# A two-layer decoder on one core: normalisation, transfer and filler steps moved in a hand-written order

## The chip, the cores and the metric

The kernel runs on one core of a Trainium2 chip. The metric is the device time of one execution in microseconds (us), lower is better. The core has five engines with a queue each, which run side by side and wait for each other by semaphores: TensorE (PE; its weight loads are shown as PEld), VectorE (DVE), ScalarE (ACT), GpSimd (POOL), and SyncE (SP), which here only issues transfers.

## The reference

Eight sequences of 112 tokens with 512 features go through two pre-normalised layers, all in float32. In outline:

```
x = x + L0_attn(layernorm(x))        # 32 query heads, 8 key heads, rotary, a sink logit per head
x = x + L0_xattn(layernorm(x), mask, ctx)   # own attention with a mask, and 375 context rows, gated
x = x + L0_ffn(layernorm(x))         # router: 8 experts, the best 2 for each token, weighted
x = x + L1_attn(layernorm(x))        # 16 query heads, 4 key heads, low-rank keys and values, anchors
x = x + L1_xattn(layernorm(x), ctx)  # softmax over the context, readout
x = x + L1_ffn(layernorm(x))         # sigmoid/tanh/sine features, two rounds of products and norms
```

In layer 1 the values are `h @ Wv_down.T @ Wv_up.T + v_anchor` and the attention output is multiplied by `Wo`. In the router the logits are `rsqrt(mean(x^2)) * x @ router_logits`, and the two largest choose the experts.

## The kernel before, in words

The 896 tokens are held as 7 tiles of 128 tokens (`NT`), and as 4 units of 2 sequences (`NU`). A Python list, `build_order()`, is the order of the whole program. A step is a tuple such as `("kq1", 0, 5)`, and each engine runs its own part of each step in the list's order: TensorE its products, VectorE and ScalarE the reading of PSUM, GpSimd some sums, SyncE the loads. Nothing reorders at run time. An instruction that waits holds up all that is behind it on its engine. `place()` goes through the list and gives each product one of the eight PSUM banks, the longest unused; the product then waits until the last reader of that bank has finished.

Steps that matter here:

- `stats`, `scale`, `turn` are a layer norm: mean and variance on VectorE (lines 1516 to 1520), the power -0.5 on GpSimd (L2251), the scaling on VectorE (L1529), the transposes on TensorE (L1053), their copy on ScalarE (L2041). In layer 0 a `scale` of a later tile also brings a bias sum `bo` on GpSimd (L2256).
- Layer 0 attention, `attend0`: `s0` scores, `m0` maxima, `p0` transposes of the weights (their copies on VectorE are L1589), `v0` values (L1119), `d0` sums. `spread` puts the projections of the next unit, `kq0` and `vp0`, between them.
- Cross attention, `attendx` and `cross`: for each sequence and group of heads `xk` computes shifted context scores (L1209); it needs the query with the maximum added, which is `mt` (a transpose on TensorE, L1199, then a sum on VectorE, L1641). `ce` are the exponentials on ScalarE (L2109), `xcv` the products with the values (L1239), `xu` the copy (L2121), `xd` and `xn` the division on VectorE (L1649 to L1666). `xw` is the output product of a tile (L1247).
- `ent` steps (L1459) are products of two weight matrices that depend on no token. They are laid where TensorE would wait. Those of layer 0 stand at the end of the cross attention, around the router (`route`, `lt`, `rank`) and before the experts.
- Router: `lt` needs a small power on GpSimd (L2331), beside eight memsets (L2330). After `rank` the tokens are scattered by transfer (`put`), and the experts' rows are loaded.
- After the experts, `get` gathers each tile's two expert rows by an indirect transfer (L2347), `mix` adds them to x on VectorE (L1827).
- Layer 1 attention: `kq1` are the eight query projections of a unit (L1381), read by VectorE (L1545) and summed by GpSimd; `ba`, `wp`, `bb` (the list `absorb()`) multiply the value-up matrix and the anchor into the output weights (L1365, L1355). `attend1` holds `s1` (scores, L1394), `c1` (L1842, L1848, exponentials L2161), `p1` (transposes; copies L2169 on ScalarE and L1864 on VectorE), `v1` (values, L1414; copies L2175 and L1870), `w1` (output, L1426). `td`, `vp1`, `ku` (L1330, L1346, L1338) are the low-rank projections.
- Loads of layer 1: `w1q` n is slot n of the query weights (1 MB, for `kq1` 2n and 2n+1), `w1o` n one quarter of the output weights (1 MB). SyncE issues `w1q` 1 when the gathers of tile 1 have landed, waits until those of tile 3 have landed, issues `w1q` 2, and then the four `w1o`.

## Time and profile before

| what | value |
|---|---|
| median of 3 runs | 1756.43 us (1752.63, 1756.43, 1756.64) |
| the profiled execution, its own time | 1756.78 us |
| its span on the core | 1754.5 us, so 2.3 us lie around it |
| TensorE busy | 1700.0 us, 97% |
| VectorE, ScalarE, GpSimd busy | 56%, 31%, 26% |
| granted TensorE clock, mean | 0.996 |
| moved from and to HBM | 155.46 MB read, 16.52 MB written |

TensorE is busy nearly all the time, so the table says little of where time could be won: one has to look for the few stretches in which TensorE waits, and for those in which its clock is granted at half. A row of the timeline has the start, the length, the engine, the line, what is written and read, the number of instructions, and in brackets the idle time before it with what ended it. The trace counts a float32 product as two matmul records: a step of 16 products shows as x32.

### The profile page before, as it was taken

The numbers are of one execution on the slowest core, as the hardware profiler recorded it, in microseconds if no ns is written. First come the engines' busy times: TensorE is split into PE (matmuls) and PEld (weight loads), VectorE is DVE, ScalarE is ACT, GpSimd is POOL, SyncE is SP. The second block draws the span as 40 slices with busy tenths as digits, with TensorE's granted clock in tenths as the row PEclk, the third lists the DMA queues.
The fourth block names the chain that finished last, engine by engine and source line by source line (L and its number), as shares of the span: only waits on it lengthen the run. The fifth ranks groups of instructions, "written<-read, shape, count | busy, mean of one in ns | idle before, by whom it ended". The sixth has DMA issues, their size and how long they took to land.

```text
span 1754.5 us, 32913 instructions
## 1 busy us (share of the span) xinstructions
PE 1700.0 (97%) x13868; PEld 1137.6 (65%) x13868; DVE 986.4 (56%) x1901; ACT 548.0 (31%) x1515; POOL 458.5 (26%) x549
## 2 busy tenths in 40 slices
PE   7999999999999999999999999998999999999998
PEld 6876666657666666666546888877677775444444
DVE  3765556437777777677743111116554555664987
ACT  0343333524444444445410111110422222333411
POOL 2532323512222213222113000005231210002676
PEclk9999999999999999999989999999999999999999
DMA  9100012000000000000147988866000033752101
GB/s 394 49 1 1 1 43 73 1 27 19 13 8 19 4 17 20 8 13 1 67 171 294 347 334 335 335 231 229 2 1 1 1 137 129 241 189 84 29 14 42
DMA packets 31987, 172.26 MB, mean 98 GB/s; under 512 B 4024, under 2 KB 4024, under 8 KB 18176
## 3 DMA queue, kind: packets, MB, share of 16 engines
q1 hardware_dynamic: 29600, 162.82, 24.9%
q0 software_dynamic: 2240, 7.34, 1.2%
q8 instruction: 109, 1.79, 0.4%
q14 instruction: 38, 0.31, 0.1%
HBM read 155.46 MB, written 16.52 MB: 98 GB/s over the span
## 4 chain that ended last, share of the span: by engine, by line
PE 86%; DVE 10%; POOL 1%; issue 1%; ACT 1%; DMA 1%; POOLq 0%; DVEq 0%; ACTq 0%
PE PS L1312 9%; PE PS L1080 7%; PE PS L1131 6%; PE PS L1381 5%; PE PS L1459 5%; PE PS L1169 5%; PE PS L1490 4%; PE PS L1321 4%; PE PS L1426 4%; PE PS L1192 3%; PE PS L1209 3%; PE PS L1477 3%; PE PS L1139 3%; PE PS L1156 2%; PE PS L1161 2%; DVE R L1618 2%
## 5 line engine op out<-in xcount | busy, mean ns | idle before, releaser
L1312 PEld LDWEIGHTS PS<-R,W 128*128 128x128 f32 x1344 | 153.2, 192 | 11.7 <-issue 11.7
L1312 PE MATMUL PS<-R,W 128*128 128x128 f32 x1344 | 153.6, 275 | 2.2 <-DVE R L1811 2.2
L1634 DVE TENSOR_REDUCE nmw<-PS 112x2 f32<-112x750 f32 x128 | 114.1, 934 | 42.5 <-PE PS L1192 42.5
L2251 POOL TENSOR_TENSOR rstd<-veps,mhalf 128x1 f32<-128x1 f32 (+1 forms) x71 | 53.8, 757 | 307.2 <-DVE veps L1520 284.0
L1080 PE MATMUL PS<-xT,W 128*128 128x224 f32 x640 | 127.8, 360 | 1.0 <-ACT xT L2041 0.7
L1080 PEld LDWEIGHTS PS<-xT,W 128*128 128x128 f32 x640 | 122.2, 194 | 9.9 <-issue 7.6
L1818 DVE TENSOR_TENSOR R<-R,PS 128x512 f32<-128x512 f32 x21 | 14.5, 688 | 199.1 <-PE PS L1312 199.1
L1459 PE MATMUL PS<-W 128*128 128x512 f32 x256 | 119.8, 611 | 0.9 <-ACT R L2109 0.9
L2109 ACT ACTIVATE R<-PS 125x672 f32<-125x672 f32 x128 | 86.6, 730 | 85.8 <-PE PS L1209 85.8
L2277 POOL TENSOR_TENSOR R<-R 128x224 f32<-128x224 f32 x80 | 52.8, 661 | 223.4 <-DVE R L1545 116.6
L1381 PE MATMUL PS<-xT,W 128*128 128x224 f32 x512 | 101.9, 359 | 2.5 <-DVE R L1545 2.2
L1490 PE MATMUL PS<-W,xT 128*128 128x512 f32 x224 | 100.7, 593 | 0.9 <-ACT xT L2046 0.9
L1381 PEld LDWEIGHTS PS<-xT,W 128*128 128x128 f32 x512 | 97.2, 193 | 5.1 <-DVE R L1545 2.5
L1131 PE MATMUL PS<-W,R 128*32 128x512 f32 (+1 forms) x512 | 99.1, 594 | 0.0
L2057 ACT ACTIVATE R<-PS,small 112x112 f32<-112x112 f32 x256 | 87.0, 386 | 34.0 <-DVE small L1569 34.0
L1602 DVE TENSOR_TENSOR x<-x,PS 128x512 f32<-128x512 f32 x35 | 24.1, 687 | 120.0 <-PE PS L1131 69.2
L1459 PEld LDWEIGHTS PS<-W 128*128 128x128 f32 x256 | 48.7, 195 | 55.5 <-issue 52.6
L2347 POOL DMA_INDIRECT R<-ys_rows,R x14 | 13.4, 958 | 245.9 <-DMA ys_rows<-R 241.6
L2271 POOL TENSOR_TENSOR R<-R,small 112x448 f32<-112x448 f32 x32 | 42.8, 1336 | 132.0 <-DVE small L1580 132.0
L1426 PE MATMUL PS<-W,R 128*32 128x512 f32 (+1 forms) x384 | 74.8, 594 | 0.7 <-DVE R L1870 0.7
L1321 PE MATMUL PS<-W,R 128*128 128x512 f32 x168 | 75.4, 592 | 0.0
L1131 PEld LDWEIGHTS PS<-W,R 128*32 128x32 f32 (+1 forms) x512 | 35.7, 130 | 60.9 <-issue 60.9
(306 smaller groups left out, 3325.3 us busy)
## 6 DMA issues: line engine op xcount, KB each, us to landing
W<-in_we SPq DMA_DIRECT2D x63, 1024.0 KB, 8.0
R<-in_ctxT SPq DMA_DIRECT2D x12, 750.0 KB, 7.3
W<-in_entwT SPq DMA_DIRECT2D x8, 1024.0 KB, 7.0
W<-in_entpw SPq DMA_DIRECT2D x8, 1024.0 KB, 8.3
R<-in_ctx SPq DMA_DIRECT2D x8, 750.0 KB
xs_rows<-in_x SPq DMA_DIRECT2D x3, 1792.0 KB, 36.1
R<-xs_rows SPq DMA_DIRECT2D x21, 256.0 KB, 8.3
ys_rows<-R SPq DMA_DIRECT2D x21, 256.0 KB, 8.5
```

The costliest lines, as they stand in the source:

```text
L1080: o = e.matmul(PS[:, m, ab * UT:(ab + 1) * UT], lw, xT[:, k, tok], start=k == 0, stop=k == 3)
L1131: o = e.matmul(PS[to, m, :], OT[:, g, c, of], Wo[:, g * 8 + c, :], start=c == 0, stop=c == 7)
L1169: o = e.matmul(PS[0:KC, m, 0:256], CT[b % 2][:, k, t * KC:(t + 1) * KC], Wx[2][:, k, 256 * g:256 * g + 256], start=k == 0, stop=k == 3)
L1312: o = e.matmul(PS[:, m, c * 128:(c + 1) * 128], gate_up(j % 3, k, off + c * 128), BT[:, j % 2, k, :], start=k == 0, stop=k == 3)
L1321: o = e.matmul(PS[:, m, :], GA[:, j % 2, k, :], W[:, GROUPS[j % 3][2], k * D:(k + 1) * D], start=k == 0, stop=k == 3)
L1381: o = e.matmul(PS[:, m, ab * UT:(ab + 1) * UT], Wlq[c // 2][:, c % 2, k, ab * 128:ab * 128 + 128], xT[:, k, tok], start=k == 0, stop=k == 3)
L1426: o = e.matmul(PS[to, m, :], LOT[:, g, c, of], Wlo[2 * g + c // 3][:, c % 3, :], start=c == 0, stop=c == 5)
L1459: o = e.matmul(PS[:, m, :], W[:, wt, kk * D + m * 128:kk * D + (m + 1) * 128], W[:, pw, kk * D:(kk + 1) * D], start=k in starts, stop=k + ...
L1490: o = e.matmul(PS[:, m, :], xT[:, k, tcol(t)], wk[:, k, :], start=k == 0, stop=k == 3)
L1634: e.tensor_reduce(nmw[0:S, par, :].rearrange("p (r f) -> p r f", r=4)[:, r:r + 2, 16 - 16 * par], PS[0:S, r:r + 2, 0:SC], AX.X, ALU.max, n ...
L2057: e.activation(SS[0:S, z, k * S:k * S + S], PS[0:S, r, bcol(j)], ACT.Exp, bias=sm[:, 1, k:k + 1], accum_out=sm[:, 4, k:k + 1])
L2109: e.activation(p_of(b, c, par)[0:KC, r:r + 2, :], PS[0:KC, r:r + 2, 0:3 * S], ACT.Exp).then_inc(*up("cexp", (b, c, par, r)))
```

## The change

Five places of the order move; each instruction that computes something is still there, except that the two-step `xw` has two waits in the place of one.

1. Layer 0 attention: `scale` of tiles 4, 5 and 6 come later, between the projections, and no longer directly behind their `stats`.
2. End of the cross attention: the last `mt` comes ahead of `xd`; only one `ent` step in the place of three stands between the last values and the output product; the output product of tile 6 waits for the last piece only before its fourth product; `scale` of tile 5 comes behind the output product. The `ent` steps that were ahead now stand behind `rank`.
3. Router: GpSimd's power comes ahead of its eight memsets.
4. Start of layer 1: `w1o` 2 and 3 are issued right behind `w1q` 1, ahead of the wait for the gathers; `ba` and the first `wp` come ahead of the transposes of tiles 2 and 3, and the next two `wp` between `kq1` 5 and 6.
5. Layer 1, unit 1: the norm of tile 6 comes behind `c1`, no longer between `s1` and `c1`.

The diff, without its context:

```
-        out += runs[n]
+        final = n == 16 * NBATCH - 1
+        out += runs[n][:-1] + [("mt", *pieces_of(n // 4), 1)] + runs[n][-1:] if final else runs[n]
...
-        if n % 4 == 3:
+        if n % 4 == 3 and not final:
...
-    at_end = {("xk", 7, 3, 1): h[:1], ("xcv", 7, 3, 1): h[1:4], ("xd", 7, 3): [("scale", 2, 5)], ("xw", 6): h[4:5] + [("turn", 2, 5)] + h[5:6] + [("route", 1)]}
+    at_end = {("xk", 7, 3, 1): h[:1], ("xcv", 7, 3, 1): h[1:2], ("xw", 6): [("scale", 2, 5)] + h[2:3] + [("turn", 2, 5)] + h[3:4] + [("route", 1)]}
...
-    ... ("route", 2), ("lt",)] + part([3]) + [("rank",)]
-    out += part(range(4, FRONT)) + ...
+    ... ("route", 2), ("lt",)] + part([2]) + [("rank",)]
+    out += part(range(3, FRONT)) + ...
...
 def pace1(step):
+    if step[0] in ("stats", "scale"):
+        return 0.0
...
-            nxt = norms(0, bs) + nxt[:4] + turns(0, bs) + nxt[4:]
+            nxt = [("stats", 0, b) for b in bs] + nxt[:1] + [("scale", 0, bs[0])] + nxt[1:2] + [("scale", 0, b) for b in bs[1:]] + nxt[2:4] + turns(0, bs) + nxt[4:]
...
-    out += [("load", "w1q", 1), ("mix", 0), ...
-    out += [("load", "w1q", 2)] + [("load", "w1o", n) for n in range(4)] + ...
+    out += [("load", "w1q", 1), ("load", "w1o", 2), ("load", "w1o", 3), ("mix", 0), ...
+    out += [("load", "w1q", 2)] + [("load", "w1o", n) for n in range(2)] + ...
...
-    out += kq[3:4] + [("mix", 5)] + kq[4:5] + turns(3, (2, 3))
-    out += [("mix", 6)] + kq[5:7] + once[:4] + begin[:-1] + kq[7:] + begin[-1:] + [("load", "mu", 0)]
+    out += kq[3:4] + [("mix", 5)] + kq[4:5] + once[:2] + turns(3, (2, 3))
+    out += [("mix", 6)] + kq[5:6] + once[2:4] + kq[6:7] + begin[:-1] + kq[7:] + begin[-1:] + [("load", "mu", 0)]
...
-            nxt = norms(3, bs) * (u > 0) + nxt[:5] + turns(3, bs) + nxt[5:]
+            nxt = nxt[:5] + turns(3, bs) + nxt[5:]
...
+        steps = [s for n in range(2 * (u == 0), 4) for s in attend1(4 * u + n)]
+        if u and u + 2 < NU:
+            k = steps.index(("c1", u, 0, 1)) + 1
+            steps[k:k] = norms(3, bs)
+        out += spread(steps, nxt, pace1)
...
                 w.wait_ge(*at("d_q3", "wx"))
-                for b in (t, t + 1):
-                    w.wait_ge(*at("oxt", (b, 3)))
-                xw_part(t, m, range(4)).then_inc(*up("attended", ("xw", t)))
+                w.wait_ge(*at("oxt", (t, 3)))
+                if t == NT - 1:
+                    w.wait_ge(*at("oxt", (t + 1, 2)))
+                    xw_part(t, m, range(3))
+                w.wait_ge(*at("oxt", (t + 1, 3)))
+                xw_part(t, m, range(3 * (t == NT - 1), 4)).then_inc(*up("attended", ("xw", t)))
...
             def ba():
-                w.wait_ge(*at("d_w1o", 3))
+                w.wait_ge(*at("d_w1o", 1))
...
             def lt():
                 w.wait_ge(*at("var", 0))
+                e.tensor_tensor(rt[:, 8, 8:8 + NT], rt[:, 8, 0:NT], mhalf[:, 0:NT], ALU.pow).then_inc(*up("rms", 0))
                 for n in range(8):
                     e.memset(rsl(rt, 9)[:, :, n:n + 1], 8.0 - n).then_inc(*up("rank", n))
-                e.tensor_tensor(rt[:, 8, 8:8 + NT], rt[:, 8, 0:NT], mhalf[:, 0:NT], ALU.pow).then_inc(*up("rms", 0))
```

The `ba` step waits for all four `w1o` loads before and now, since they count up one semaphore; only the last in order is another. Line numbers of the changed kernel are 7 to 10 higher from the output product on.

TensorE at the start of layer 1. Before, the transposes of tiles 2 and 3 (`xn` into PS, 8 transposes) follow the five projections, and `ba` (`W,col`) and `wp` (`W` alone) come behind two more projections:

```order
L1381 MATMUL PS<-xT,W 128x224 x40
L1053 MATMUL PS<-cst,xn 128x128 x8
L1381 MATMUL PS<-xT,W 128x224 x16
L1365 MATMUL PS<-W,col 32x512 x16
L1355 MATMUL PS<-W 32x512 x12
L1394 MATMUL PS<-R 112x112 x16
```

The same stretch in the changed kernel:

```order
L1391 MATMUL PS<-xT,W 128x224 x40
L1375 MATMUL PS<-W,col 32x512 x16
L1365 MATMUL PS<-W 32x512 x4
L1060 MATMUL PS<-cst,xn 128x128 x8
L1391 MATMUL PS<-xT,W 128x224 x8
L1365 MATMUL PS<-W 32x512 x8
L1391 MATMUL PS<-xT,W 128x224 x8
L1404 MATMUL PS<-R 112x112 x16
```

Twenty products moved ahead of the transposes and eight between the projections; the sum of the stretch is the same.

VectorE at the end of the cross attention, from the division of the last group but one (`xd`) on. Before, the sum with the query (L1641, `R,PS` 128x112) stands behind the four instructions of the division:

```order
L1649 TENSOR_SCALAR R<-R,cst 128x224
L1651 SCALAR_TENSOR_TENSOR R<-R,cst 128x224
L1654 STREAM_SHUFFLE R<-R 128x224
L1656 RECIPROCAL R<-R 128x224
L1641 TENSOR_TENSOR R<-R,PS 128x112
```

In the changed kernel it stands ahead of them:

```order
L1651 TENSOR_TENSOR R<-R,PS 128x112
L1659 TENSOR_SCALAR R<-R,cst 128x224
L1661 SCALAR_TENSOR_TENSOR R<-R,cst 128x224
L1664 STREAM_SHUFFLE R<-R 128x224
L1666 RECIPROCAL R<-R 128x224
```

One instruction changed its place with four.

VectorE at the first scores of unit 1 of layer 1. Before, the norm of tile 6 (its last instruction is the scaling, `xn<-x,mv,rstd`) stands ahead of the reading of the scores (L1842) and of a copy for TensorE (L1864):

```order
L1516 BN_STATS st<-x 128x6
L1518 BN_AGGR mv<-st 128x2
L1520 TENSOR_SCALAR veps<-mv 128x1
L1529 TENSOR_SCALAR xn<-x,mv,rstd 128x512
L1842 TENSOR_TENSOR R<-PS,cst 112x896
L1864 COPY R<-PS 112x448
```

In the changed kernel:

```order
L1852 TENSOR_TENSOR R<-PS,cst 112x896
L1874 COPY R<-PS 112x448
L1858 TENSOR_REDUCE ls<-R 112x8
L1860 TENSOR_SCALAR ls<-ls 112x8
L1526 BN_STATS st<-x 128x6
L1528 BN_AGGR mv<-st 128x2
L1530 TENSOR_SCALAR veps<-mv 128x1
L1539 TENSOR_SCALAR xn<-x,mv,rstd 128x512
```

The four instructions of the norm went behind the four that read the scores and the transposed weights.

## Rows read from the trace of the kernel before

**Rows 1.** Part 1 of the page: busy time, share, instructions of each engine.
```profile
PE 1700.0 (97%) x13868; PEld 1137.6 (65%) x13868; DVE 986.4 (56%) x1901; ACT 548.0 (31%) x1515; POOL 458.5 (26%) x549
```

**Rows 2.** Timeline, layer 0 attention: start, length, engine, instruction [idle before].
```profile
72.09 1.41 DVE L1529 TENSOR_SCALAR xn<-x,mv,rstd 128x512 f32<-128x512 f32 x1 [0.52 <-POOL rstd L2251]
...
74.09 0.97 PE L1119 MATMUL PS<-R 112*64 112x448 f32 x4 [1.30 <-DVE R L1589]
```

**Rows 3.** Timeline, end of the cross attention and the router.
```profile
882.02 0.32 PE L1199 MATMUL PS<-cst,nmw 112*128 112x112 f32 x1
...
884.92 0.21 DVE L1641 TENSOR_TENSOR R<-R,PS 128x112 f32<-128x112 f32 x1
...
885.18 0.92 PE L1209 MATMUL PS<-R 32*125 32x112 f32 x24 [0.82 <-DVE R L1641]
...
886.98 3.78 PE L1459 MATMUL PS<-W 128*128 128x512 f32 x4 [0.88 <-ACT R L2109]
...
892.11 0.54 ACT L2121 ACTIVATE R<-PS 128x448 f32<-128x448 f32 x1 [4.56 <-PE PS L1239]
...
896.24 0.34 DVE L1666 SCALAR_TENSOR_TENSOR R<-R,tg 128x112 f32<-128x112 f32 x1
...
904.96 0.35 POOL L2330 MEMSET R<- 128x7 f32 x8 [1.12 <-DVE R L1686]
```

**Rows 4.** Windows: stretch, length, busy by engine, granted clock, DMA share, GB/s.
```profile
882.20:886.20 4.00, 2.36 (x65) 1.63 (x64) 3.52 (x9) 1.34 (x3) 2.17 (x3) 1.00 0.20 84
886.20:893.10 6.90, 6.12 (x30) 2.74 (x31) 0.38 (x2) 1.89 (x3) 0.00 (x0) 0.51 0.01 4
...
910.10:913.50 3.40, 3.40 (x5) 1.32 (x4) 2.89 (x14) 0.05 (x1) 0.00 (x0) 0.51 1.00 422
...
1220.70:1224.20 3.50, 3.50 (x11) 3.18 (x10) 3.46 (x5) 0.00 (x0) 1.82 (x3) 0.51 0.02 7
```

**Rows 5.** Timeline, start of layer 1.
```profile
1199.81 15.40 PE L1381 MATMUL PS<-xT,W 128*128 128x224 f32 x80
...
1216.70 0.66 PE L1053 MATMUL PS<-cst,xn 128*128 128x128 f32 x4 [1.05 <-DVE R L1545]
...
1218.38 1.14 DVE L1545 TENSOR_TENSOR R<-PS,cst 128x448 f32<-128x448 f32 x2
...
1219.58 8.01 PE L1381 MATMUL PS<-xT,W 128*128 128x224 f32 x32 [2.22 <-DVE R L1545]
...
1227.52 3.64 PE L1365 MATMUL PS<-W,col 128*32 128x512 f32 x32
...
1230.97 2.82 PE L1355 MATMUL PS<-W 128*32 128x512 f32 x24
```

**Rows 6.** SyncE's issues, and DMA from 1188 to 1222: packets, windows, us to landing.
```profile
1188.82 11.61 SPq L2406 DMA_DIRECT2D W<-in_w1q  x2
...
DMA packets 738, 3.39 MB, mean 212 GB/s; under 512 B 126, under 2 KB 126, under 8 KB 522
...
1212.00:1216.00 4.00, 3.65 (x21) 3.36 (x20) 3.34 (x9) 0.32 (x1) 2.68 (x5) 1.00 1.02 424
...
1218.00:1222.00 4.00, 2.42 (x9) 2.28 (x10) 3.96 (x7) 0.00 (x0) 1.76 (x3) 0.84 0.32 78
...
W<-in_w1q SPq DMA_DIRECT2D x1, 1024.0 KB, 8.4
R<-ys_rows,R POOLq DMA_INDIRECT x8, 8.8
```

**Rows 7.** Timeline, layer 1, first scores of unit 1.
```profile
1294.31 4.95 POOL L2261 TENSOR_TENSOR x<-x,R 128x512 f32<-128x512 f32 x4
...
1299.87 0.55 DVE L1529 TENSOR_SCALAR xn<-x,mv,rstd 128x512 f32<-128x512 f32 x1 [5.34 <-POOL rstd L2251]
...
1302.00 0.78 PE L1414 MATMUL PS<-R 112*32 112x112 f32 x24 [1.12 <-DVE R L1864]
...
1306.65 1.02 PE L1346 MATMUL PS<-W,xT 128*112 128x96 f32 x8 [1.25 <-ACT R L2175]
```

More of the change, by code:

```diff
@@ L403, in experts @@
 def experts():
-    out = [("load", "front", 3), ("load", "we", 0), ("load", "w1s", 0), ("scale", 2, 6), ("turn", 2, 6), ("route", 2), ("lt",)] + part([3]) + [("rank",)]
-    out += part(range(4, FRONT)) + [("ea", 0, k) for k in range(FRONT)] + [("put", t) for t in range(NT)]
+    out = [("load", "front", 3), ("load", "we", 0), ("load", "w1s", 0), ("scale", 2, 6), ("turn", 2, 6), ("route", 2), ("lt",)] + part([2]) + [("rank",)]
+    out += part(range(3, FRONT)) + [("ea", 0, k) for k in range(FRONT)] + [("put", t) for t in range(NT)]
     out += [("load", "experts", 0), ("load", "rows", 0), ("load", "we", 1), ("load", "rows", 1), ("load", "rows", 2), ("load", "we", 2)]
@@ L579, in build_order @@
             out += norms(3, (4, 5)) + once[4:10] + second + once[10:]
-        out += spread([s for n in range(2 * (u == 0), 4) for s in attend1(4 * u + n)], nxt, pace1)
+        steps = [s for n in range(2 * (u == 0), 4) for s in attend1(4 * u + n)]
[3 more added lines that the diff above has]
+        out += spread(steps, nxt, pace1)
     out += [("load", "c5", 0), ("load", "c5", 1), ("mu",)]
```

4 lines of the change are left out of this document (2 added, 2 removed).

## The prediction, as put on record before the run

> **What bounds the kernel now.** I read the page's busy shares first. TensorE works 1700.0 us of a 1754.5 us span, 97% [rows 1], so 54.5 us are all that any reordering can win, and some of those lie at the start and the end. Then I went through TensorE's waits in order of time, since in a stream as full as this each wait that goes moves all that is behind it, unless the next wait grows by as much. Third I read the granted clock by windows, as a busy TensorE at half clock is lost time too, which no list of waits shows. The reader is to see two things: the changed places are exactly places where TensorE waits 0.8 to 2.2 us for an engine whose queue holds something less urgent in front [rows 2, 3, 5, 7]; and just behind two of them the clock is granted at 0.51, the lower of its levels (1.2 in the place of 2.4 GHz) [rows 4].
>
> **Layer 0, scaling between the projections.** TensorE's values wait 1.30 us for a VectorE copy. In front of that copy stand two scalings, the second of which starts at 72.09 and takes 1.41 us, up to 73.50, and TensorE goes on at 74.09 [rows 2]. Without them the copy comes more than 1.4 us sooner, so the whole 1.30 goes. The scalings now run between projections. There VectorE follows TensorE and the transposes that need them stand four projections later. With each goes a sum of 128x512 on GpSimd, 1.24 us by the four of that shape in 4.95 us [rows 7]; it may hold up one rotary sum by less than that, hidden by the 3.08 us that a projection takes (five in 15.40 us) [rows 5]. Bounds: a gain of 0 to 1.30; I take 1.30. The move of tile 6 meets no wait of TensorE and is worth 0.
>
> **End of the cross attention.** The maxima are transposed at 882.02 to 882.34, but VectorE adds them only at 884.92, behind the division, and TensorE waits 0.82 us until 885.18 [rows 3]. Now the sum is first: it is ready near 882.7, and the division starts some 0.3 to 0.5 later, with its result needed only at the output product. The wait of 0.82 goes; the wait of 0.88 behind it, for an exponential [rows 3], stays, since it hangs on the same products.
>
> Then the filler: three `ent` steps before the output product become one. The path there is copy, division, last product: from 892.11 to 896.24 + 0.34 = 896.58, thus 4.47 us [rows 3], less one scaling that has left it. What TensorE has to do in that time is one `ent` (4 records) and three quarters of the output product (6 records). Four records take 3.78 us at half clock [rows 3], so 0.47 each at full clock, and ten take 4.7. That covers 4.47 with 0.2 to spare. Without the split there would be 1.9 us of cover and 2.6 of waiting; so the two-step product pays for the filler that left. Cost 0; bounds 0 to 0.5 lost. The two steps that left are done later, in front of the experts, where they give the scatter and the rows' load more room; TensorE does not wait there, so this is worth 0. The memsets that GpSimd does now after its power take 0.35 us [rows 3], beside products and copies that are needed first: 0, at most 0.35 either way.
>
> **Start of layer 1.** The transposes of tile 3 wait 1.05 us and the sixth projection waits 2.22 us, both for VectorE to empty a bank (L1545), which stands behind the mixing of the tiles [rows 5]. Put in front of them now are `ba`, 3.64 us, and one `wp`, a third of 2.82, so 0.94 [rows 5]. The five projections end at 1199.81 + 15.40 = 1215.21. Then `ba` ends at 1218.85 and `wp` at 1219.8. The transposes take banks that VectorE releases at 1218.38 + 1.14 = 1219.52, and ScalarE by its copy of `ba`; the sixth projection takes the bank of `wp`, copied during the transposes. So 1.05 + 2.22 = 3.27 us go, with margins of 0.3 us or less, for which I keep 0.3 of loss in the sum.
>
> This needs the loads. `ba` waits for all four `w1o`, 12 us sooner than before (1215.2 against 1227.5). In the 16 us from 1188 the queues moved 3.39 MB, 212 GB/s, while they can do 424 [rows 6]; there is room for another 3.4 MB and the two early loads are 2.1 MB, 4.9 us at the full rate. The old burst fades out in 1218 to 1222, with a share of 0.32 of 4 us, so it ends near 1219.3 at the latest [rows 6]; 4.9 earlier is 1214.4. That is 0.8 before `ba`. The third query slot is issued by 1188.82 + 11.61 = 1200.43 and lands 8.4 us later, at 1208.8 [rows 6]; the fifth projection wants it at 1199.81 + 4 x 3.08 = 1212.1: 3.3 us of slack for gathers that are slowed by the early loads. I take 0 for both.
>
> **Layer 1, unit 1.** The power for tile 6 stands on GpSimd behind four sums of 4.95 us, and VectorE waits 5.34 us for it [rows 7]. Behind that wait stand the reading of the scores and a copy; so TensorE waits 1.12 for the copy and 1.25 for a ScalarE copy behind the late exponentials [rows 7]. With the norm behind them the exponentials start about those 5.34 us earlier. Both waits go: 2.37. The VectorE wait for the power remains, but what is then behind it is the sum of an output product that ends about when the wait does. The normed tile is wanted only after the low-rank products. Bounds 1.1 to 2.4; I take 2.37.
>
> **The clock.** In 882.2 to 886.2 TensorE worked 2.36 of 4.00 us, and then its clock was at 0.51 for 6.90 us, in which it worked 6.12 [rows 4]: at the full clock half of that, 3.0 us, would be saved. After the two waits at 1216 to 1219.6 it was at 0.51 for 3.50 us of full work: 1.7 us. With the waits gone the second fall should go surely (TensorE is then busy throughout). For the first only 0.82 of the 2.4 us of waits goes, so it may fall still; I count it as gone with some doubt. The fall at 910.10 in the router [rows 4] follows tiny products that the change leaves as they are, and stays. Bounds: 0 to 4.7; I take 4.7.
>
> The Trainium skill speaks against this part: TensorE: Matmul & The Clock Gate, in "What's actually happening", makes the slow level follow an idle stretch of the engine, not a merely thinner one. Row and rule differ here: the falls came after waits of at most 0.9 and 2.2 us [rows 3, 5], with work between them. By that rule, they have a cause that the change does not touch, and the time would be the 1749.7 of the first rival below.
>
> **The sum.** 1.30 + 0.82 + 3.27 + 2.37 = 7.76 us of waits, and 4.7 of clock, less 0.7 for small new waits (0.3 at the transposes, 0.4 at the output product and elsewhere) is 11.8. The profiled execution took 1756.78 us (1754.5 of span and 2.3 around it), 0.35 above the median of 1756.43. 1756.78 - 11.8 = 1745.0. Its own range: 1743 to 1747.
>
> **Rivals.**
> - The clock falls as before. A thinner stretch remains in front of the first fall, and it could be due to what TensorE does there and not to the waits. If both falls stay, the time is 1756.78 - 7.76 + 0.7 = 1749.7, with the first alone 1748.0. For it: at 910.10 the clock fell with no long wait [rows 4]. Against: the second follows the largest wait within the program. Chance 0.24, time 1749.
> - The early loads cost what they were to save. The gathers share the queues with 2.1 MB; if they are later by the full 4.9 us, the third slot lands at 1213.7 and the fifth projection waits 1.6, and `ba` may wait until 1219.3, another 2.5, with the clock's 1.7 not won. 1745.0 + 5.8 = 1750.8, in the middle 1748 to 1751. For it: gathers take 8.8 us to land already [rows 6]. The Trainium skill, DMA: Bandwidth & Descriptors, "Queues, rings and completion order", has each DMA engine take turns between the queues it has work for; the gathers would then lose up to half their rate while the loads run. Chance 0.14, time 1750.
> - It does not do what it says: each wait that goes turns up at the next thing that the same slow engine owes (VectorE with its mixing, ScalarE with its exponentials), and less than 5 us is left: 1751.5 to 1757. For it: VectorE works 3.52 of 4 us and 3.96 of 4 at two of the places [rows 4, 6]. Against: what comes next there waits for TensorE, not the other way. Chance 0.11.
> - Slower. The mechanism is starvation of the gathers: two 1 MB loads directly ahead of them, where SyncE formerly held back. From a landing of the third slot at 1212.1 on, each microsecond costs one; at 17 late, 1229, it costs all of the gain and 5 more: 1762. It would take gathers of 29 us in the place of 8.8 [rows 6], which only a queue that lets the loads go entirely first, twice over, would give. Chance 0.05.
>
> **How the numbers follow.** Forecast 0.46, then 0.24, 0.14, 0.11, 0.05. 0.3% is 5.3 us, about what a measurement of this kernel tells from no change, so faster means below 1751.2: the first three, less a tail where the loads cost more, 0.81. Within 0.3%: 0.13. Slower: 0.06. The range takes in the first three with their bounds, from 1742 (no new waits, and a little more clock) to 1752.
>
> **What would show it.** In the profile after: no wait for L1589's successor near 73; the context product near 884 starting without a wait for VectorE's sum; `ba` starting where the transposes did, without a wait for a transfer; no granted clock of 0.51 near 1217; unit 1's values without waits of 1.1 and 1.2. A wait of TensorE for `W<-in_w1q` or `W<-in_w1o`, or the clock at half at the same two places, would make the forecast wrong.

## The result, and the profile after

The changed kernel takes 1742.56 us (median of four executions, 1739.89 to 1744.11), the kernel before 1756.54 beside it on the same chip: ratio 0.9923, 95% interval 0.9904 to 0.9943. The forecast was 1745.0 in a range of 1742 to 1752. A second study of the same program, told below, gave 1742.67 and 0.9924 (0.9910 to 0.9937). The profiled execution took 1741.91 us, 14.87 less than the one before, so 3.1 more than the 11.8 forecast. In two of the studies below one execution ran far slower, at a mean granted clock of 0.75 and 0.85 (2176.89 us in run 1, 1956.18 in run 6); the ratios leave it out, and the medians would be 0.1 us lower without it.

Part 1 of the page of the changed kernel; it answers to [rows 1]. Line numbers are up to 10 higher than before (L1126 was L1119, L1391 was L1381):

```profile
PE 1692.8 (97%) x13868; PEld 1134.6 (65%) x13868; DVE 987.1 (57%) x1901; ACT 547.8 (31%) x1515; POOL 459.1 (26%) x549
```

TensorE's busy time fell by 7.2 us for the same 13868 records of products: that part of the gain is time at a higher clock and, as shown below, time lost inside the records. Only the other 7.2 us of the span's 14.4 were idle time before.

Timeline of the changed kernel, layer 0 attention, the values that had waited and the projections behind them (start, length, engine, instruction, idle before). It answers to [rows 2]:

```profile
71.77 1.34 PE L1126 MATMUL PS<-R 112*64 112x448 f32 x5
...
73.42 9.35 PE L1087 MATMUL PS<-xT,W 128*128 128x224 f32 x48
...
82.16 1.77 POOL L2281 TENSOR_TENSOR R<-R,small 112x448 f32<-112x448 f32 x1
...
84.08 0.95 PE L1116 MATMUL PS<-cst,R 112*112 112x112 f32 x8 [0.53 <-POOL R L2281]
```

The wait of 1.30 is gone, and a new one of 0.53 for a GpSimd product stands 10 us behind.

Timeline, end of the cross attention, answering to [rows 3]:

```profile
879.54 0.27 DVE L1651 TENSOR_TENSOR R<-R,PS 128x112 f32<-128x112 f32 x1 [0.16 <-PE PS L1206]
...
881.47 0.92 PE L1216 MATMUL PS<-R 32*125 32x112 f32 x24
...
883.26 1.98 PE L1469 MATMUL PS<-W 128*128 128x512 f32 x4 [0.88 <-ACT R L2119]
...
887.71 3.79 PE L1254 MATMUL PS<-W,R 128*128 128x512 f32 x8
```

VectorE's sum comes directly behind the transpose (which ends at 879.51) and not 2.6 us behind it; the wait of 0.82 is gone, 0.88 stays, and four `ent` records take 1.98 us where they took 3.78. (A third wait, of 0.73 us for an exponential, stands ahead of these two in every trace; the change leaves it as it is.) The output product runs in one piece of 3.79 us with no wait shown.

Windows of the changed kernel over both places where the clock had been low in [rows 4], and over the router (length, busy by engine, granted clock, DMA share, GB/s):

```profile
879.00:883.30 4.30, 2.69 (x78) 1.89 (x70) 3.84 (x10) 2.21 (x5) 2.22 (x3) 1.00 0.30 120
883.30:890.00 6.70, 6.70 (x38) 3.00 (x38) 3.30 (x8) 1.08 (x2) 1.59 (x2) 1.00 0.00 1
...
899.80:903.20 3.40, 3.40 (x6) 1.43 (x6) 2.76 (x13) 0.00 (x0) 0.00 (x0) 0.50 1.01 426
...
1211.40:1214.80 3.40, 3.40 (x30) 2.20 (x23) 3.37 (x6) 2.24 (x4) 1.74 (x2) 1.00 0.00 0
```

Two of the three low stretches inside the span are gone; the router's is there.

Timeline, start of layer 1, answering to [rows 5]:

```profile
1193.11 15.40 PE L1391 MATMUL PS<-xT,W 128*128 128x224 f32 x80
1208.44 3.64 PE L1375 MATMUL PS<-W,col 128*32 128x512 f32 x32
...
1212.87 1.09 PE L1060 MATMUL PS<-cst,xn 128*128 128x128 f32 x8
1213.79 3.19 PE L1391 MATMUL PS<-xT,W 128*128 128x224 f32 x16
```

There is no idle time between any two rows of this stretch, for VectorE or for a transfer.

Timeline, layer 1, unit 1, answering to [rows 7]:

```profile
1288.37 1.36 PE L1424 MATMUL PS<-R 112*32 112x112 f32 x48
1289.65 1.73 PE L1340 MATMUL PS<-xT,W 128*64 128x224 f32 x8
1291.31 1.81 PE L1356 MATMUL PS<-W,xT 128*112 128x96 f32 x16
```

Both waits are gone, and the values and the low-rank product run in one piece each.

**Where the time went, in one table.** All traces here have 13868 records of products on TensorE, and outside the edited places in the same order. So the start of one and the same record in two traces says how far one kernel is ahead there. I took the lead over the kernel before at eight places and wrote down how it grew between them, in us; the start of the span (up to 1.5) is left out. The last column lists the stretches with a granted clock of 0.5 inside the span, by their start, before the end of the kernel; "x2" is a stretch of twice the length (6.8 us for 3.4).

```
place, in before's time   60-100  100-118  118-880  880-947  947-1260 1260-1308 1308-1740  low clock at
before                       -       -        -        -        -         -         -      886 x2, 910, 1221
changed                    1.65    1.10     0.04     3.80     5.09      2.82     -0.01     900
changed, second profile    1.66    1.08    -0.04     2.14     5.09      2.81      0.00     898 x2
scalings of 4, 5 alone     1.65    0       -0.22     1.16    -0.21      0        -3.34     886, 906, 1217, 1306 x2
scaling of 6 alone         0.01    1.08     0.01    -0.44     1.78      0         0        885, 906 x2
maxima first alone         0       0       -1.53     3.66     1.46      0.01     -3.32     747, 907, 1303 x2
norm of tile 6 alone       0.01    0       -0.05     0.06    -0.12      2.82      0.01     885 x2, 909, 1220
loads and absorb alone     0.01    0        0.18    -0.14     4.11      0.01      0        886 x2, 910
absorb undone              1.66    1.08    -1.56     5.17     0.09      2.82      0.03     746, 1213
loads undone               1.64    1.09    -1.19     3.80    -2.27      2.82      0.01     723, 901, 1211 x2
one step undone            1.65    1.09    -1.55    -0.47     5.03      2.81      0.02     746, 893, 906
more scalings              1.64    1.09     1.75     5.18     4.77      2.82      0.03     none
same, bias sum later      -0.64   -0.10     1.61     3.79     5.07      2.82      0.01     98, 901
same, one step            1.66    1.09     1.47    -0.47     4.24      2.81      0.01     890, 904
```

### The profile page after: what moved, and what is told of

Its sections match the earlier page's. It is cut to its first block, busy times and chain, and to the rows that moved or that the text cites. A ratio compares the mean times of both kernels' runs of the same rounds, so it can differ in the third digit from the quotient of the medians.

```text
span 1740.1 us, 32912 instructions
## 1 busy us (share of the span) xinstructions
PE 1692.8 (97%) x13868; PEld 1134.6 (65%) x13868; DVE 987.1 (57%) x1901; ACT 547.8 (31%) x1515; POOL 459.1 (26%) x549
## 4 chain that ended last, share of the span: by engine, by line
PE 87%; DVE 8%; POOL 1%; issue 1%; ACT 1%; DMA 1%; POOLq 0%; DVEq 0%; ACTq 0%
PE PS L1322 9%; PE PS L1087 6%; PE PS L1391 6%; PE PS L1138 6%; PE PS L1469 5%; PE PS L1176 5%; PE PS L1500 4%; PE PS L1436 4%; PE PS L1331 4%; PE PS L1199 3%; PE PS L1216 3%; PE PS L1487 3%; PE PS L1146 3%; PE PS L1163 2%; PE PS L1168 2%; DVE R L1628 2%
## 5 line engine op out<-in xcount | busy, mean ns | idle before, releaser
L1322 PEld LDWEIGHTS PS<-R,W 128*128 128x128 f32 x1344 | 153.2, 192 | 11.7 <-issue 11.7
L1828 DVE TENSOR_TENSOR R<-R,PS 128x512 f32<-128x512 f32 x21 | 14.4, 688 | 199.1 <-PE PS L1322 199.1
L1391 PE MATMUL PS<-xT,W 128*128 128x224 f32 x512 | 100.4, 355 | 0.2 <-ACT xT L2051 0.2
L1391 PEld LDWEIGHTS PS<-xT,W 128*128 128x128 f32 x512 | 95.7, 190 | 3.2 <-issue 2.6
```

The lines of the kernel that those rows point to most:

```text
L1322: o = e.matmul(PS[:, m, c * 128:(c + 1) * 128], gate_up(j % 3, k, off + c * 128), BT[:, j % 2, k, :], start=k == 0, stop=k == 3)
L1391: o = e.matmul(PS[:, m, ab * UT:(ab + 1) * UT], Wlq[c // 2][:, c % 2, k, ab * 128:ab * 128 + 128], xT[:, k, tok], start=k == 0, stop=k == 3)
```

## Experiments

**1. The scalings of tiles 4 and 5 alone**, on the kernel before:

```
+            later = [("stats", 0, b) for b in bs] + nxt[:1] + [("scale", 0, bs[0])] + nxt[1:2] + ...
+            nxt = (later if u == 0 else norms(0, bs) + nxt[:4]) + turns(0, bs) + nxt[4:]
```

> The kernel before with one part alone: the scalings of tiles 4 and 5 between the projections of layer 0. Theory (a wait of TensorE is partly hidden in the trace, because a record of a product ends later than the next product could have started): the first output product (start 117.69 before) comes 1.7 us earlier, 2.3 won near 75 and 0.6 given back to GpSimd near 84; span shorter by 1.7. Rival (the idle time that the trace shows is the whole wait): 1.30 won and 0.5 given back, 0.8 us. Neither expects a change of the clock.

Measured: 1755.52 us, ratio 0.9991 (0.9981 to 1.0001). Behind 75 (in before's time) it has won 2.3 us, behind 84 there are 1.65 left. The new wait comes with this edit (timeline):

```profile
84.00 0.95 PE L1110 MATMUL PS<-cst,R 112*112 112x112 f32 x8 [0.54 <-POOL R L2272]
```

So 1.65 us, not the 1.30 that the trace shows as idle, and 0.6 of the 2.3 are given back. The interval of the ratio (3.3 us faster to 0.2 slower) has room for 1.65 and for nothing. The profiled execution is slower than the median (1757.87 us): it has a double low stretch at 1306 that the one before had not, behind waits that both have.

**2. The scaling of tile 6 alone** (the same two lines with `u == 1`):

> The kernel before with one part alone: the scaling of tile 6 later in layer 0, where the trace of before showed no idle time of TensorE. Theory (hidden waits): the output product at 117.69 comes 1.1 us earlier. Rival (no idle time shown, so nothing to win): 0.0 us. In both the rest is unchanged; a time of one run cannot tell 1 us, the starts in the trace can.

Measured: 1756.62 us, ratio 0.9995 (0.9985 to 1.0004), which tells nothing of one microsecond. The trace does: 1.08 us are won where the trace of before shows no idle time. Timeline of this kernel:

```profile
114.34 1.34 PE L1120 MATMUL PS<-R 112*64 112x448 f32 x5
115.15 0.54 PE L1120 MATMUL PS<-row,R 112*64 112x448 f32 x1
...
115.99 1.55 PE L1132 MATMUL PS<-W,R 128*128 128x512 f32 x3
```

From the first of the values to the next group are 1.65 us here. The same products in the trace of the kernel before:

```profile
114.94 2.07 PE L1119 MATMUL PS<-R 112*64 112x448 f32 x6
116.84 0.91 PE L1119 MATMUL PS<-row,R 112*64 112x448 f32 x2
117.69 0.70 PE L1131 MATMUL PS<-W,R 128*128 128x512 f32 x1
```

There it is 2.75 us, with groups that touch each other. Most of the difference is no pause at all. `v0` writes two heads into two halves of 64 PSUM partitions, and the records of two heads start together when the inputs of both are there. If the second copy is late, the first head's records run by themselves. Timeline of a short window at the first of the values, first of this kernel, then of the kernel before:

```profile
114.34 0.60 PE L1120 MATMUL PS<-R 112*64 112x448 f32 x2
```

```profile
114.94 0.59 PE L1119 MATMUL PS<-R 112*64 112x448 f32 x1
```

In this kernel all eight records start in four pairs, 0.38 to 0.43 us apart. Before, two pairs and four single records take six such steps: the two steps more are 0.8 of the 1.1 us. The rest is a pause. A record is drawn with 0.54 us while the next step starts after 0.38, so 0.16 of a pause is covered by the record before it, and idle time under 0.15 us is not listed. At the place of run 1 the same working gives 1.30 shown + 0.16 covered + 0.8 for heads that ran singly, which is the 2.3 us won there.

**3. The maxima first, alone** (`mt` ahead of `xd` in the last run; the output product in one step, the three `ent` steps in their place):

```
+        final = n == 16 * NBATCH - 1
+        out += runs[n][:-1] + [("mt", *pieces_of(n // 4), 1)] + runs[n][-1:] if final else runs[n]
-        if n % 4 == 3:
+        if n % 4 == 3 and not final:
```

> The kernel before with one part alone: the last maximum's step ahead of the division at the end of the cross attention. Theory (the clock falls because TensorE's waits lie close together): the wait of 0.82 goes, 1.6 of 2.4 us of waits stay, and the clock stays up near 886, so the first product of the experts (945.90 before) comes 3.8 us earlier, 0.9 by the wait and 2.9 by the clock. Rival (the fall has a cause that the waits do not touch): the clock is at half for some 6.9 us as before, and the gain is 0.9 us.

Measured: 1754.69 us, ratio 0.9986 (0.9975 to 0.9996); 3.66 us won between 880 and 947, 0.82 of them the wait. The changed kernel wins 3.80 there, so the rest of parts 2 and 3 of the change (filler, split, GpSimd's power), which was not run by itself, makes 0.14 in sum. Window of this kernel in the stretch that answers to 886 to 893 in [rows 4]:

```profile
888.00:895.60 7.60, 7.60 (x41) 3.69 (x41) 3.75 (x8) 0.54 (x1) 1.59 (x2) 1.00 0.00 0
```

The clock stays up with one of the waits gone; that is 2.8 of the 3.66 us. The 0.73 and 0.88 that stay were not enough for a fall in any trace: all five kernels with all three waits (before, runs 1, 2, 4, 5) have a low stretch at 885 or 886, and none of the seven profiles with those two alone has it (run 3, the changed kernel twice, runs 6, 7, 9, 10).

**4. The norm of tile 6 later in layer 1, alone:**

```
-            nxt = norms(3, bs) * (u > 0) + nxt[:5] + turns(3, bs) + nxt[5:]
+            nxt = nxt[:5] + turns(3, bs) + nxt[5:]
+            k = steps.index(("c1", u, 0, 1)) + 1
+            steps[k:k] = norms(3, bs)
```

> The kernel before with one part alone: the norm of tile 6 behind the reading of the scores in unit 1 of layer 1. Theory: the two waits at 1302 and 1306 go and with what was hidden in the records 2.7 us are won by 1310 and kept to the end. Rival (the waits shown are all): 2.4 us; second rival (they turn up again behind ScalarE's exponentials): under 1 us.

Measured: 1753.72 us, ratio 0.998 (0.997 to 0.999), and 2.82 us in the table: the two waits of 1.12 and 1.25 [rows 7] cost 0.45 more than is shown (about 0.17 each is covered by the record before the wait). Everything else is as before, down to the low stretches.

**5. Loads and absorbed products together, alone** (the lines of the change on `w1q`, `w1o`, `once` and the wait of `ba`, nothing else):

> The kernel before with only two edits of the start of layer 1 together: the first two output weight loads ahead of the third query slot, and the absorbed products ba and wp between the projections, ahead of the second pair of transposes. Theory (the two edits need one another, and the rest of the change has no part in it): waits of 1.05 and 2.22 us near 1216 and 1219 go, and with them the fall of the granted clock near 1220 (1.7 us): 5.0 us less than before, 1751.5 us, ratio 0.9971; the changed kernel's own step there was 5.1 us between 1215 and 1234. Rival (the clock falls there anyway, at a place set by the time since the last change and not by the waits): 3.3 us, 1753.3 us, ratio 0.9981. Second rival (without the earlier stages' gain the loads come late): a wait for the transfer at L1375 of 1 us or more, 1754 us or more.

Measured: 1752.2 us, ratio 0.9971 (0.9957 to 0.9985). In the trace 4.11 us and no low clock at 1221. Of the 1.0 that is missing, 0.82 is a wait that the changed kernel does not have:

```profile
1215.97 3.64 PE L1365 MATMUL PS<-W,col 128*32 128x512 f32 x32 [0.82 <-DMA W<-in_w1o]
```

So the second rival of this run holds in part, but not for its reason. SyncE's issues and `ba` move together: from the issue of `w1q` 1 to the end of the five projections it is 26.4 us here and 26.3 in the changed kernel. What differs is how long the last two loads take to land (lines from a view of their tile, first of this kernel, then of the changed one):

```profile
DMA to landing us min/median/max: 9.8/11.6/13.5
```

```profile
DMA to landing us min/median/max: 9.1/10.8/12.4
```

In the changed kernel the last load was issued at 1195.9 and landed 12.4 us later, at 1208.3, and `ba` started at 1208.44: there was 0.1 us to spare. In run 10 it took 11.7 us, and in run 11, below, 13.7, with the wait there too. Of the seven profiles with both edits (run 5, the changed kernel twice, runs 8 to 11) two have this wait. Why the landing varies was not tried. The five medians alone give 1.1 + 0.0 + 1.9 + 2.9 + 5.6 = 11.5 us (each against the kernel before in its own study); the whole gave 14.0. The first two of these differences are within the noise.

**6. The changed kernel with the absorbed products back behind the transposes**, the loads still early:

```
-    out += kq[3:4] + [("mix", 5)] + kq[4:5] + once[:2] + turns(3, (2, 3))
-    out += [("mix", 6)] + kq[5:6] + once[2:4] + kq[6:7] + begin[:-1] ...
+    out += kq[3:4] + [("mix", 5)] + kq[4:5] + turns(3, (2, 3))
+    out += [("mix", 6)] + kq[5:7] + once[:4] + begin[:-1] ...
```

> The changed kernel with one part undone: the transposes of tiles 2 and 3 are again ahead of ba and the wp steps; the early loads stay. Theory: the waits of 1.05 and 2.22 us come back, and the clock falls to half just behind them for some 3.4 us, so that the first scores of layer 1 come 5.0 us later than in the changed kernel (1221.99). Rival (clock falls do not hang on these waits): 3.3 us later, with the clock at 1.00 there.

Measured: 1746.85 us, ratio 0.9938 (0.9920 to 0.9956). Nothing is won between 947 and 1260 (0.09). The waits and the low clock are back (timeline and window):

```profile
1210.08 0.66 PE L1060 MATMUL PS<-cst,xn 128*128 128x128 f32 x4 [0.99 <-DVE R L1555]
1212.97 8.01 PE L1391 MATMUL PS<-xT,W 128*128 128x224 f32 x32 [2.23 <-DVE R L1555]
```

```profile
1213.40:1216.80 3.40, 3.40 (x12) 3.04 (x11) 3.33 (x6) 0.00 (x0) 2.23 (x3) 0.51 0.00 0
```

**7. The changed kernel with all four output weight loads behind the third query slot:**

```
-    out += [("load", "w1q", 1), ("load", "w1o", 2), ("load", "w1o", 3), ("mix", 0), ...
-    out += [("load", "w1q", 2)] + [("load", "w1o", n) for n in range(2)] + ...
+    out += [("load", "w1q", 1), ("mix", 0), ...
+    out += [("load", "w1q", 2)] + [("load", "w1o", n) for n in range(4)] + ...
```

> The changed kernel with one part undone: all four loads of the output weights again behind the wait for the gathers. Theory (the early loads are needed, ba would come before its weights): TensorE waits 2 to 3 us for a transfer near 1208.4, the clock may fall behind it, 2 to 4.5 us slower in all. Rival (the order of the products alone does it, loads come soon enough): no wait for a transfer, no difference, within 0.3 us at the first scores.

Measured: 1748.66 us, ratio 0.9948 (0.9932 to 0.9963). The wait is twice what the theory had (2 to 3 us). Timeline and window:

```profile
1213.45 5.96 PE L1375 MATMUL PS<-W,col 128*32 128x512 f32 x32 [4.92 <-DMA W<-in_w1o]
```

```profile
1211.50:1218.20 6.70, 4.75 (x24) 1.35 (x28) 5.95 (x9) 0.00 (x0) 3.46 (x4) 0.50 0.06 15
```

The absorbed products without the loads are worse than neither: a wait of 4.92 us and a double low stretch, 7.4 us behind the changed kernel (5.09 + 2.27). The loads alone (run 6) win nothing. Each edit is worth something only with the other.

**8. The changed kernel with tile 6's output product in one step:**

> The changed kernel with one part undone: the output product of tile 6 waits for everything before its first product. Theory: it stands idle for what the three first products covered, about 2.3 us, near 888 to 890; with the waits of 0.7 and 0.9 ahead the clock falls again, so 2.3 us by the wait and 1.7 to 3 by the clock. Rival (the division is done early enough, the split is worth nothing): under 0.3 us.

Measured: 1747.6 us, ratio 0.9943 (0.9928 to 0.9958). Timeline and window:

```profile
891.74 0.70 PE L1254 MATMUL PS<-W,R 128*128 128x512 f32 x1 [2.51 <-DVE R L1673]
```

```profile
889.10:892.50 3.40, 0.89 (x3) 0.49 (x3) 2.41 (x4) 0.00 (x0) 1.35 (x2) 1.00 0.00 0
892.50:896.00 3.50, 3.50 (x5) 1.35 (x4) 0.00 (x0) 0.00 (x0) 0.00 (x0) 0.51 0.00 0
```

The prediction had put 2.6 us of waiting on this without the split; 2.51 are there, and the low clock behind them costs 1.8 more: 3.80 + 0.47 = 4.3 us in the table.

**9. More of the same: the scalings of tiles 0 and 1 for the cross attention** between the projections of layer 0's last unit, where the changed kernel still waits:

```
-            nxt = norms(1, (0, 1)) + nxt[:4] + turns(1, (0, 1)) + norms(1, (2,)) + ...
+            nxt = [("stats", 1, 0), ("stats", 1, 1)] + nxt[:1] + [("scale", 1, 0)] + nxt[1:2] + [("scale", 1, 1)] + nxt[2:4] + turns(1, (0, 1)) + norms(1, (2,)) + ...
```

> The changed kernel and one step more of the same kind: in the last but one unit of layer 0 the scalings of the next stage's tiles 0 and 1 too come between the projections, where TensorE waits 1.39 us at 202.09. Theory: with the hidden part 2.2 us are won there and kept; span about 1737.9 for 1740.1. Rival (only what is shown): 1.4 us. Second rival: the wait turns up again at a GpSimd or VectorE step behind it, as 0.5 us did at 84.

Measured: 1739.64 us, ratio 0.9904 (0.9890 to 0.9917), below both kernels. Timeline of the changed kernel, and then of this one, for the same values:

```profile
199.73 0.97 PE L1126 MATMUL PS<-R 112*64 112x448 f32 x2
202.09 0.97 PE L1126 MATMUL PS<-R 112*64 112x448 f32 x4 [1.39 <-DVE R L1599]
```

```profile
199.97 1.79 PE L1126 MATMUL PS<-R 112*64 112x448 f32 x6
...
202.43 4.13 PE L1138 MATMUL PS<-W,R 128*128 128x512 f32 x9
```

At this place 1.5 us are won (from the first of the values to the next group 4.01 us become 2.46), 1.75 up to 880. The theory's 2.2 did not come: the first head's records still run singly here (the row of 1.79 us), and the free stream would take 1.65 in all. Of the 2.6 us between the two spans, the router gives 1.4 more, since its low stretch is missing in this execution, as it is in that of run 6, although its products are the same, and 0.5 are lost at the start and between 947 and 1260.

**10. Run 9, with GpSimd's bias sum behind the rotation products** of its tile:

```
-            def scale(st_, b):
+            def turn(st_, b):
                 if st_ == 0 and b >= 2 * UB:
                     bo(b)
...
```

> The kernel with three more scalings interleaved (1739.64 us median) and, in addition, GpSimd's bias sum of a tile (bo, 1.26 us on GpSimd) issued after the tile's rotation products and not ahead of them. In the trace of the changed kernel bo stood on GpSimd from 79.70 to 80.96 and the product R<-R,small that TensorE waits for began at 82.16 beside VectorE's scaling of a tile, took 1.77 us instead of 1.31 to 1.37, and TensorE waited 0.53 us at 84.08; the kernel lost 0.61 us of its lead there. Theory (the late GpSimd product is bo's doing): the wait at 84.08 goes, 0.6 us are won, some 1739.0 us, ratio to before 0.9901. Rival (the product is slow because it runs beside VectorE's scaling, whatever GpSimd did before it): the wait stays at 0.4 to 0.6 us, 1739.6 us. Second rival (the bias sums collide with the next unit's rotation products): a new wait of about 1 us on L1116 or L1107, 1740.5 us or more.

Measured: 1743.25 us, ratio 0.9919 (0.9905 to 0.9932): worse than run 9 by 0.0015 of the ratio, 2.6 us (the medians are 3.6 apart, but come from two studies in which the kernel before differs by 1.5). The traces have 3.5 us lost in 60 to 118. Timeline of this kernel:

```profile
80.74 1.77 POOL L2281 TENSOR_TENSOR R<-R,small 112x448 f32<-112x448 f32 x1
81.19 0.53 DVE L1539 TENSOR_SCALAR xn<-x,mv,rstd 128x512 f32<-128x512 f32 x1
...
82.66 0.95 PE L1116 MATMUL PS<-cst,R 112*112 112x112 f32 x8 [0.43 <-POOL R L2281]
...
92.89 2.88 POOL L2266 TENSOR_TENSOR x<-x,row 128x512 f32<-128x512 f32 x2
...
95.73 0.93 POOL L2281 TENSOR_TENSOR R<-R,small 112x448 f32<-112x448 f32 x1
...
96.81 0.95 PE L1116 MATMUL PS<-cst,R 112*112 112x112 f32 x8 [1.88 <-POOL R L2281]
```

The first wait shrinks from 0.53 to 0.43 only: the product takes 1.77 us with no bias sum in front of it, so it is slow beside VectorE's scaling, as the rival had it. And both bias sums now stand, 2.88 us, in front of the product for the next heads; TensorE waits 1.88, and the clock is low behind it:

```profile
98.70:102.10 3.40, 3.40 (x46) 2.14 (x40) 1.43 (x3) 0.01 (x1) 0.00 (x0) 0.54 0.00 0
```

Both rivals were right and the theory fell. The product at 95.73 takes only 0.93 us: it comes so late that VectorE's own product for the same heads is over (more on that in the last section).

**11. Run 9 with the output product in one step** (runs 8 and 9 together, to have the wait of run 8 at another time of the program):

> The kernel with three more scalings interleaved (1739.64 us median, no fall of the clock inside its span), but with the output product of tile 6 in cross-attention in one step again, as before. Everything up to there runs 1.5 us earlier than in the changed kernel with the one step undone, so this is the same wait at another time. Theory (the fall follows the wait): TensorE idles 2.5 us near 889 as there, and the granted clock falls to 0.5 within some us of it: 2.3 us of wait and 3.3 us of clock, 1744.6 to 1745.2 us, ratio 0.993. Rival (the fall of the clock there was set by the time at which the kernel reached the place): the wait alone, 2.3 us, 1741.9 us, ratio 0.9917, with no stretch of 0.5 between 880 and 915.

Measured: 1744.68 us, ratio 0.9919 (0.9903 to 0.9936). Timeline and window:

```profile
889.17 3.09 PE L1254 MATMUL PS<-W,R 128*128 128x512 f32 x4 [2.51 <-DVE R L1673]
```

```profile
890.10:893.50 3.40, 3.40 (x5) 1.35 (x4) 0.00 (x0) 0.00 (x0) 0.00 (x0) 0.53 0.00 0
```

With the same 2.51 us of waiting, 2.6 us earlier in the span, the clock fell again. In the two profiles with this wait, runs 8 and 11, the fall follows it. It may not be so in each execution: one of the four of run 11 took 1741.74 us at a mean granted clock of 0.998, where the profiled one had 0.997 and the rival's price was 1741.9.

This trace also has the late load of run 5, though the kernel was 3.6 us ahead of the one before when it got there. Run 8, only 1.0 ahead, has no such wait:

```profile
1212.36 3.64 PE L1372 MATMUL PS<-W,col 128*32 128x512 f32 x32 [0.76 <-DMA W<-in_w1o]
```

**12. The changed kernel, not edited, a second time:**

> The changed kernel itself once more, nothing edited: its instructions and waits are known, so what differs in the profile is not the program's doing. Theory (a fall of the granted clock needs waits of TensorE just before it, but which of the places with waits shows one changes from execution to execution): the waits repeat within 0.1 us, the one stretch at 0.51 near 900 may be missing or another may be there (near 746, where all kernels have waits of 0.2 and 1.0 us, or near 906), the span is 1738 to 1744 us and the single times differ by 3 us or more. Rival (the place of a fall is fixed by the program): one stretch of 3.4 us near 899.8 and none elsewhere within the span, and single times within 1 us of each other. Either way the median should be 1742.5 us, ratio 0.992, which also says whether the kernel with three more scalings interleaved (0.9904) is really below it.

Measured: 1742.67 us (1741.98 to 1746.41), ratio 0.9924 (0.9910 to 0.9937). Its leads grow as in the first profile, within 0.1 us, at every place but one: the router, where this time the stretch is twice as long, from 897.88. Window:

```profile
897.00:904.00 7.00, 6.68 (x19) 4.32 (x20) 3.12 (x15) 0.42 (x2) 0.00 (x0) 0.56 1.00 424
```

That is 1.66 us (3.80 against 2.14), with not one instruction changed. The theory held in part: no stretch was missing and none was elsewhere, but how long it lasted was not the program's doing. Run 9's ratio lies below both of the changed kernel's, but the intervals overlap; of its 3.0 us of median the trace gives 1.7, and for the rest the clock differed: its mean was 0.999 in three of run 9's five executions and 0.997 in three of this kernel's five.

## Why the prediction was right, point by point

- **Layer 0, tiles 4 and 5: forecast 1.30, measured 2.3, then 0.6 back** (run 1). The mechanism was right, the size not: the step took the idle time in the row as the price of the wait, and left out the heads that ran singly because of it (0.8 us). The bound of 1.30 that I gave as the highest was too low.
- **Layer 0, tile 6: forecast 0, measured 1.1** (run 2). "Meets no wait of TensorE" was read from rows that list no idle time. The loss was in records that ran one after another instead of in pairs (0.8), and in a pause too short to be listed. This is the clearest miss.
- **Bias sums on GpSimd: "hidden by the 3.08 us that a projection takes".** Not so: the product behind them takes 1.77 us beside VectorE's scaling, not 1.31, and TensorE waits 0.53. Run 10 shows that it is for the most part the neighbour on VectorE and not the bias sum in front: with the sum moved away the loss is 0.5 us in the place of 0.6. The reserve of 0.7 for small new waits, put elsewhere, was used up here (0.6).
- **Cross attention: forecast 0.82 + 3.0, measured 3.80.** Runs 3 and 8 show both halves: the sum placed first takes away 0.82 and with it the low clock, and the product in two steps keeps 2.51 us of waiting and a new low stretch from coming. The cover, forecast as 4.7 against 4.47, sufficed.
- **Start of layer 1: forecast 3.27 + 1.7 = 4.97, measured 5.09.** The loads were in time, and the margins of 0.3 held. But the landing came out with 0.1 us to spare, where my sum (1214.4 against 1215.2) had 0.8, and in runs 5 and 11 the same loads were 0.82 and 0.76 late. It is not the gain of the earlier stages that makes the difference (run 8 had 1.0 us of it and did not wait, run 11 had 3.6 and did). That the loads were in time in the profile that was to be forecast is luck in part. In run 7 the trace shows the price of late loads. I took the harm to the gathers as 0, and it is not: see the last section. The 3.3 us of slack of the third query slot covered it.
- **Unit 1: forecast 2.37, measured 2.82** (run 4); the 0.45 are again more than the idle time listed.
- **The clock: forecast 4.7 won at two places, measured both.** The rival with the clock as before (1749.7) is refuted at 886 by run 3, and at 1221 by run 5 and by the changed kernel: none of the seven profiles in which the two waits there are gone has a fall near it, while the larger wait of run 7 brought one back. The Trainium skill, TensorE: Matmul & The Clock Gate, "What's actually happening", ties the slow level to an idle stretch; the windows of run 8 show it after one in which TensorE had worked 0.89 of 3.40 us, and [rows 4] after one with 2.36 of 4.00. For these places the rows decide against the narrow reading: no complete idleness was needed.
- But "with the waits gone the second fall should go surely" says less than it seems. The same two waits near 1217 stand in six kernels here. The clock fell behind them in four (before, runs 1, 4 and 6) and not in two (runs 2 and 3). Window of run 2, the waits and what followed:

```profile
1216.00:1219.40 3.40, 1.17 (x7) 1.17 (x7) 3.33 (x6) 0.60 (x1) 2.24 (x3) 1.00 0.40 101
1219.60:1222.90 3.30, 3.30 (x20) 3.30 (x19) 3.26 (x6) 0.00 (x0) 1.73 (x2) 1.00 0.01 3
```

- In the same way the waits of 1.12 and 1.25 near 1300 cost 3.3 us of clock in runs 1 and 3 and nothing in before, 2 and 5, and the two near 744 that no edit touches (0.21 and 0.96 us in the changed kernel) have a low stretch behind them, at 1.5 to 1.6 us, in runs 3, 6 and 8 only (run 7 has one at 723 instead, behind waits of 0.63 and 0.17).
- So the gain of unit 1 is, on average, more than its 2.82 us, since a possible fall goes with the waits; the sum had no term for that. And that the profile of the changed kernel has no fall at 746, where runs 6 and 8 lose 1.5 us with the same waits, is luck that the sum did not price.
- **The sum.** 11.8 was forecast and 14.9 measured between the two profiles: 1.0 + 1.1 + 0.45 that no row lists as idle make 2.5 of the 3.1, the rest is 0.1 at the start of layer 1, 0.1 of unused reserve and 0.4 at the two ends of the kernel. The rivals on late loads, on waits that turn up elsewhere, and on starved gathers did not come true as wholes. Of the first there are the 0.8 us of runs 5 and 11, of the second the 0.53 on GpSimd, of the third 1.2 us that cost TensorE nothing. The median of 1742.56 lies only 0.6 inside the stated range and below the forecast's own range of 1743 to 1747: the small terms left out all pointed one way.

What stays open: why the clock falls behind some waits in one execution and not in the next. Run 12 shows that the program does not decide it alone; what does was not tried. Open too is what makes the last load land 11.7 to 13.7 us after its issue. The Trainium skill, TensorE: Matmul & The Clock Gate, "What's actually happening", says of the slow time at a kernel's start that it varies from run to run; that a fall in the middle does is shown by run 12 (3.4 and 6.8 us).

## What to carry to other kernels

Price a wait by the distance between the same two products in a stream that runs freely and in the one that waits (1.65 against 2.75 us for eight records), not by the idle time that is shown. Where two products can run side by side, look whether their records start in pairs: an input that is late for one of them costs whole steps (0.4 us each here) with no idle time at all. When waits stand close together, price the clock behind them too, as something that happens in part of the executions: here it added 1.7 to 1.8 us to waits of 3.3 (run 6) or 2.5 (run 8), and 1.5 to 3.3 at other places. And an early use of data needs its early load: move both or neither, and leave room for the landing to vary: a margin of 0.1 us in one profile was 0.8 too little in two others.

## What the runs showed of the hardware

- How long a GpSimd product of 112x448 takes depends on what VectorE does beside it. In the 14 traces together there are 448 of them (`R<-R,small`). It took 0.92 to 0.93 us in the 15 cases in which VectorE's own product of the same shape was not running (run 10, 95.73); 1.31 to 1.38 in the 421 in which it overlapped with that product, which reads two inputs from SBUF; and 1.77 to 1.78 in the 12 in which a VectorE scaling of 128x512 overlapped as well (run 10, 80.74 and 81.19). Beside VectorE's copies out of PSUM it stayed at 0.93 (95.73 again). The Trainium skill, GPSIMD Engine Reference, "Specifications", has GpSimd share its ways into SBUF with VectorE where VectorE runs in a two-port mode or reads two inputs from SBUF; the step from 0.93 to 1.31 agrees with the second. Which mode the scaling ran in, and so whether its 0.4 us come from the first, was not tried.
- The granted clock fell to 0.5 with TensorE partly at work (0.89 of 3.40 us before the fall of run 8), and in two executions of one program for 3.4 and for 6.8 us at the same place.
- Two records of 112x448 that use different halves of 64 columns start within 0.01 us of each other when both inputs are there; singly, each takes a step of 0.38 to 0.43 us of its own (run 2 and the kernel before, 114 to 118).
- Two transfers of 1 MB put ahead of the gathers slow them a little. SyncE issues `w1q` 2 when the gathers of tile 3 have landed. From the issue of `w1q` 1 to that of `w1q` 2 it is 12.3 to 12.7 us in all eight profiles with the early loads, and 11.2 to 11.5 in all six without (11.3 of the 11.61 of the row at 1188.82 in [rows 6], which ends with the second issue). Timeline of the changed kernel, the two issues:

```profile
1182.26 0.33 SPq L2416 DMA_DIRECT2D W<-in_w1q  x1
...
1195.00 0.33 SPq L2416 DMA_DIRECT2D W<-in_w1q  x1
```

So the gathers of tile 3 land 1.2 us later, which TensorE does not feel.
